# An output add moved between two kinds' taps, and the last round's fillers re-dealt

## The reference

```
yc = conv(qkv);  qkv = silu(yc)
M = where(stril, (k_beta @ k.T) * decay, 0);  T = inv(I + M)
v_new = v_i - kcd_i @ state
out_i = (q_i * exp(g_i)) @ state + attn @ v_new
state = state * exp(g_last) + (k_i * exp(g_last - g_i)).T @ v_new
s = (norm_w * rms(core) * silu(z)) @ W_out.T
x + s * silu(ffn(xn))
```

## Time and profile before

| | |
|---|---|
| median of three timed runs | 2303.93 us |
| the profiled execution | 2307.89 us |
| its span, first to last instruction | 2306.1 us |
| PE, DVE, ACT, POOL busy in the span | 94%, 71%, 57%, 74% |
| mean granted TensorE clock | 0.986 |
| chain that ended last: PE, DVE, ACT, issue | 66%, 17%, 9%, 5% |

### The profile page before, as it was taken

The page is one execution under the profiler, slowest core; times in us unless marked ns, Lnnn a source line. Parts: engine busy times, 40 slices in busy tenths (PEclk is TensorE's granted clock), DMA queues, the critical chain, the costliest instruction groups (busy, mean ns, idle before and its releaser), DMA issues.

```text
span 2306.1 us, 76444 instructions
## 1 busy us (share of the span) xinstructions
PE 2178.9 (94%) x32208; PEld 1671.9 (72%) x32208; DVE 1641.1 (71%) x3307; ACT 1311.1 (57%) x3141; POOL 1709.9 (74%) x1774
## 2 busy tenths in 40 slices
PE   3799999999999999999999999999999999998898
PEld 2687777777777777777777777777777777776554
DVE  6777777777777777777777777777877677776322
ACT  3666655666566655666556555666665566664111
POOL 2787888888877888888877788888877788888100
PEclk8899999999999999999999999999999999999999
DMA  3211110111111110111111110111111102111100
GB/s 91 56 42 34 46 37 25 31 46 37 46 32 35 46 37 22 33 46 37 46 32 35 46 30 26 37 46 37 41 37 34 35 21 46 37 37 42 38 19 19
DMA packets 70951, 87.45 MB, mean 38 GB/s; under 512 B 16721, under 2 KB 39377, under 8 KB 70609
## 3 DMA queue, kind: packets, MB, share of 16 engines
q1 hardware_dynamic: 70608, 82.55, 14.0%
HBM read 77.45 MB, written 5.08 MB: 36 GB/s over the span
## 4 chain that ended last, share of the span: by engine, by line
PE 66%; DVE 17%; ACT 9%; issue 5%; POOL 2%; DMA 1%; DVEq 0%; POOLq 0%; SPq 0%; ACTq 0%
DVE cacc L1016 10%; PE ps_two L429 10%; PE ps_p L675 8%; PE ps_state L429 5%; PE ps_p L612 4%; PE ps_two L454 4%; PE ps_state L636 3%; PE ps_p L585 3%; PE ps_p L620 3%; PE ps_p L503 3%; PE ps_state L503 2%; ACT qg L790 2%; PE ps_p L724 2%; DVE acc L1281 2%; PE ps_two L664 2%
## 5 line engine op out<-in xcount | busy, mean ns | idle before, releaser
L1351 POOL TENSOR_TENSOR Sd<-St,el 128x512 f32<-128x512 f32 x192 | 201.3, 1048 | 276.6 <-DVEq L1253 276.6
L1390 POOL TENSOR_SCALAR Kg<-idx_s,lutb 128x134 f32<-128x134 int32 x480 | 355.7, 744 | 27.1
L1232 DVE TENSOR_SCALAR Vn<-ps_p,bR 128x128 f32<-128x128 f32 x512 | 168.2, 350 | 225.8 <-PE ps_p L585 151.9
L1016 DVE SCALAR_TENSOR_TENSOR cacc<-ps_state,cw,cacc 128x1022 f32<-128x1022 f32 (+2 forms) x192 | 244.4, 1273 | 15.5 <-DVE cacc L1016 7.6
L675 PE MATMUL ps_p<-w_o,hT 128*128 128x256 f32 x992 | 244.5, 390 | 7.1 <-ACT V L829 5.8
L1016 DVE SCALAR_TENSOR_TENSOR cacc<-ps_two,cw,cacc 128x1022 f32<-128x1022 f32 (+2 forms) x192 | 244.9, 1275 | 5.3 <-DVE cacc L1016 0.5
L429 PE MATMUL ps_state<-xnT,w_qkv 128*128 128x256 f32 x1024 | 234.2, 382 | 5.9 <-DVEq L1021 5.9
L429 PE MATMUL ps_two<-xnT,w_qkv 128*128 128x256 f32 x1024 | 236.4, 384 | 0.0
L429 PEld LDWEIGHTS ps_state<-xnT,w_qkv 128*128 128x128 f32 x1024 | 193.6, 192 | 32.6 <-DVEq L1021 6.3
L922 ACT ACTIVATE P<-ps_p 128x128 f32<-128x128 f32 x256 | 67.2, 277 | 260.6 <-PE ps_p L590 260.6
L675 PEld LDWEIGHTS ps_p<-w_o,hT 128*128 128x128 f32 x992 | 182.1, 191 | 43.6 <-issue 19.9
(11 more groups left out here) (195 smaller groups left out, 5388.6 us busy)
## 6 DMA issues: line engine op xcount, KB each, us to landing
qg<-g_scratch SPq DMA_DIRECT2D x64, 512.0 KB, 7.3
g_st<-g_scratch SPq DMA_DIRECT2D x64, 256.0 KB, 5.5
w_qkv<-in_wqkvz SPq DMA_DIRECT2D x16, 512.0 KB, 3.8
w_z<-in_wqkvz SPq DMA_DIRECT2D x16, 256.0 KB, 3.2
w_o<-in_wout SPq DMA_DIRECT2D x16, 256.0 KB, 2.9
idx_s<-in_idx SPq DMA_DIRECT2D x32, 67.0 KB, 1.8
fw_scratch<-looked_up SPq DMA_DIRECT2D x32, 67.0 KB, 2.7
Kg<-in_x SPq DMA_DIRECT2D x2, 1024.0 KB, 5.9
```

What stands on the lines that cost most here:

```text
L1016: dve.scalar_tensor_tensor(dst, both[n][:, :, 0:S - t], cw[:, kind, 3 - t:4 - t], dst, ALU.mult, ALU.add).then_inc(s["taps"], 1)
L1232: dve.tensor_scalar(Vn[:, cur, b], bank[:, 0:P], bR[:, R.par, b, c:c + 1], None, ALU.mult).then_inc(done, 1)
L1351: pool.tensor_tensor(Sd[:, :, :, :], St[:, c % 2, :, :, :], el[:, R.par, :, :, c].unsqueeze(3).broadcast_to([P, BB, RATIO, P]), ALU.mult). ...
L1390: m = pool.tensor_scalar(slots[k], idx_s[:, :], float(k), lutb[:, k:k + 1], ALU.is_equal, ALU.mult)
```

## The change

1. In rounds 1 to 30 DVE adds output quarter 3 between the taps of kind 2 and those of kind 3, not after them.
2. In the last round PE computes output quarters 0, 1 and 2 ahead of the first products of the inversion, and DVE adds them there. Quarter 2 goes to bank 7 and quarter 3 to bank 5; hidden unit 1, whose banks are 6 and 7, waits for quarter 2 to be read.
3. At the last round's end the four output quarters are interleaved with hidden units 3, 4 and 5 of the FFN's first group: PE computes quarters 0 and 1, unit 3, the turning of quarter 3, quarter 2, unit 4, quarter 3, and unit 5 once unit 3 has been multiplied. The quarters use banks 0 and 2 instead of 0 and 1. ACT and DVE take the units in the same order, before the loops of the FFN and DVE's wait for x.

```diff
-AHEAD = {0: 0, 1: 6, 2: 0}
+AHEAD = {0: 0, 1: 6, 2: 0, 3: 4, 4: 6, 5: 4}
+IN_LEVELS = 3
+OUT_LAST = {(5, 1): (3,)}
...
-    outs = [] if first else spread([("out", 0), ("out", 1), ("out", 2), ("ot3", 0), ("out", 3)], (5, 4, 5, 4, 4))
+    outs = [] if first else spread([("out", 0), ("out", 1), ("out", 2), ("ot3", 0), ("out", 3)], (5, 4, 5, 4, 4) if nxt else (5, 4, 7, 4, 5))
...
-    end = [] if nxt else spread([("end", i) for i in range(4)], (0, 1))
+    end = [] if nxt else spread([("end", i) for i in range(4)], (0, 2))
...
                 if R.before() is not None:
-                    outputs(R, "out", R.before(), 0)
+                    for t in range(1 if R.nxt else 3):
+                        outputs(R, "out", R.before(), t)
...
+                        if f == 1 and j == 0:
+                            wait_read(pe, R, "out", 2)
...
-                    turn_back(R, 3)
-                    for t in range(4):
-                        outputs(R, "end", R, t)
+                    outputs(R, "end", R, 0)
+                    outputs(R, "end", R, 1)
+                    for j in range(2):
+                        gate_up(3, 3, 0, j, AHEAD[3])
+                    turn_back(R, 3)
+                    outputs(R, "end", R, 2)
+                    for j in range(2):
+                        gate_up(4, 4, 0, j, AHEAD[4])
+                    outputs(R, "end", R, 3)
+                    pe.wait_ge(s["ff_h"], 4)
+                    for j in range(2):
+                        gate_up(5, 5, 0, j, AHEAD[5])
...
                 scale_last(R)
+                if not R.nxt:
+                    for f in range(IN_LEVELS, FT):
+                        gated_unit(f, f, AHEAD[f])
...
                 if of is not None:
                     gated(of, 3)
+                if R.nxt and of is not None:
                     outputs(R, "out", of, 2)
                 if R.nxt:
                     taps(R, 2, (1, 2, 3))
-                    taps(R, 3, (1, 2, 3))
                 else:
                     hidden(2, 2, AHEAD[2])
                 if of is not None:
                     outputs(R, "out", of, 3)
+                if R.nxt:
+                    taps(R, 3, (1, 2, 3))
...
                     gated(R, 2)
+                    outputs(R, "end", R, 0)
+                    outputs(R, "end", R, 1)
                     gated(R, 3)
-                    for t in range(4):
-                        outputs(R, "end", R, t)
+                    outputs(R, "end", R, 2)
+                    hidden(3, 3, AHEAD[3])
+                    outputs(R, "end", R, 3)
+                    hidden(4, 4, AHEAD[4])
+                    hidden(5, 5, AHEAD[5])
```

More of the change, by code:

```diff
@@ L557, in beside @@
                 if R.before() is not None:
-                    for t in OUT_AT.get((lv, half), ()):
+                    for t in (OUT_AT if R.nxt else OUT_LAST).get((lv, half), ()):
                         outputs(R, "out", R.before(), t)
@@ L563, in beside @@
                         if not R.nxt:
-                            pe.wait_ge(s["ff_h"], len(AHEAD))
+                            pe.wait_ge(s["ff_h"], IN_LEVELS)
                     zproj(R, i)
@@ L1196, in invert @@
                 if of is not None:
-                    outputs(R, "out", of, 0)
+                    for t in range(1 if R.nxt else 3):
+                        outputs(R, "out", of, t)
                 second_products(R, 4, 2)
@@ L1204, in invert @@
                     hidden(1, 1, AHEAD[1])
-                if of is not None:
+                if R.nxt and of is not None:
                     outputs(R, "out", of, 1)
```

## The result

The changed kernel takes 2246.77 us (median of 4 runs, 2245.33 to 2248.87), the kernel before 2304.13 us in the same comparison (2302.78 to 2312.45).

The account below looks back on a forecast made before the run. PE was taken to bound the kernel, waiting in 30 rounds for DVE's late add and stalling seven times. Terms 26.7 + 4.9 + 0 + 9.2 = 40.8 us gave 2263.1 us from the 2303.93 median; range 2248 to 2285.

Parts of the forecast that it names:

- Change 1, the stalls: Seven stalls inside `keys_through`: fetch gets ahead of the `w_qkv` load, so four even ones shrink to odd size, 4.9 us gained.
- My second rival: All seven `keys_through` stalls go, as PE's sequencer can run ahead during z products: 16.0 us, time 2252.0; chance 0.10.
- Change 1, the thirty rounds: Rounds 1 to 30: `keys_through` starts 0.97 us earlier, ACT's lateness costs 0.08; 0.89 a round, 26.7 us gained.
- Change 2: Last round's first phase: same PE work in another order, no gap to fill; 0 gained.
- Change 3: Last round's end: idle time between units and quarters filled, slow clock gone, first down product 9.2 us earlier.
- ACT in PE's place: Rounds: the recurrence's first products already hang on ACT's Kg copies, each round loses 0.07 us; time 2296.8, chance 0.10.
- More stalls: Rounds: the 0.97 us pause lets fetch keep up, without it further rounds stall 2.29 us each; up to 2320.7, chance 0.04.
- Quarter 3's bank not full: Rounds: DVE waits for PE's quarter 3, taps come late, only the end gains; 2294.7 us, chance 0.04.
- Instruction fetch: Stalls in `keys_through`: by the skill's rule of mostly hidden block crossings the stall term would be 0, time 2268.0.

Follow-up runs that it names:

- the end alone: Kernel before with only the last round's output quarters interleaved with hidden units 3 to 5: 2294.81 us, ratio 0.9963.
- gates first: Changed kernel with ACT taking the SiLU of z products 0 to 2 before the SiLU of kind 3: 2239.64 us, ratio 0.9709.
- held kernel: Any kernel whose PE waits just before `keys_through`; the kernel before with the head's transposes made three times, 128 instructions more, ran once at 2319.71 us.

## Why the prediction was wrong

- **Change 1, the stalls: the step that failed.** I wrote that the instructions "queue behind" the `w_qkv` load, and took the difference between even and odd stalls, 4.9 us; by the traces the disturbed rounds were worth 29.0. Two things were wrong, the cause and the price. The cause: the stalls come from the wait itself, and go with it, odd ones too. My second rival said so, at 0.10, and "nothing shows how far the sequencer runs ahead" was my argument against it. The traces do show it, in the DMA view of the stretch just ahead of `keys_through` in round 16. In the kernel before (1147.3 to 1149.6 us, L577 at 1149.60) only data moves, and the instruction packet comes in the stretch after the earlier trace rows:

```profile
q1 hardware_dynamic: 144, 0.07, 12.5%
```

After the change (1126 to 1128.3 us, L582 at 1128.32) the packet is there ahead of it:

```profile
q1 hardware_dynamic: 152, 0.07, 12.1%
q8 instruction: 1, 0.02, 2.4%
```

  The same holds of all seven rounds: the packet starts 1.0 to 2.7 us behind the first product of `keys_through` in the kernel before, and 1.2 to 1.7 us ahead of it in the same rounds after. When it is asked for no view shows. One case could have been read before any run: round 0 of the kernel before has no late add to wait for, and in the 1.2 us ahead of its first product (114.9 to 116.1) nothing moves but

```profile
q8 instruction: 1, 0.02, 5.6%
```

- **The price of the stalls.** Even the rival stopped at 16.0 us, the idle time that the view puts before the stalled matmul. The rounds lost 29.0, the seven alone 26.0. In round 16 of the kernel before, the half z product behind the stalled matmuls took 2.07 us where an undisturbed round has 1.12, and that second delay is in no row on L577:

```profile
1154.95 2.07 PE L454 MATMUL ps_two<-xnT,w_z 128*128 128x512 f32 x2
```

  It is the clock. PE had stood idle for 2.68 us, and as it resumes its granted clock falls from 1.00 to 0.50 (2.4 to 1.2 GHz). The stretch, in the columns of the earlier trace rows:

```profile
1153.93:1157.34 3.41, 3.32 (x31) 1.70 (x33) 0.00 (x0) 1.08 (x2) 0.00 (x0) 0.50 0.00 0
```

  Such a slow stretch stands behind five of the seven stalls, in rounds 8, 16, 24, 25 and 26. Beyond 64.07 us and its stall's idle time, each of these rounds is 1.8 to 2.1 us longer; rounds 9 and 17, whose clock stays at 1.00, are so by 0.3 and 0.4 us. From these rounds' lengths the clock's share is, by estimate, 5 x 1.5 = 7.5 us. One pair shows it alone: round 26 stalls for the same 3.00 us at the same place in the kernel before and with the end alone, but with the end alone the clock stays at 1.00, and the round takes 67.50 us instead of 69.08. The kernel before first:

```profile
1812.16 0.33 PE L577 MATMUL ps_state<-XW,Kg 64*64 64x64 f32 x3 [3.00 <-issue]
1812.41 1.83 PE L454 MATMUL ps_two<-xnT,w_z 128*128 128x512 f32 x2
```

```profile
1808.29 0.33 PE L578 MATMUL ps_state<-XW,Kg 64*64 64x64 f32 x3 [3.00 <-issue]
1808.55 1.13 PE L455 MATMUL ps_two<-xnT,w_z 128*128 128x512 f32 x2
```

  Measured from L577 to L577, as the undisturbed 64.07 us was, the price had been there to read. With it the rival gives 26.7 + 29.0 + 9.2 = 64.9 us; the two traces are 62.6 apart, the medians 57.4.

- **Change 1, the thirty rounds.** The forecast was 0.89 us a round; 0.77 was measured. The mechanism was right: L582 starts at the z products' end, the second batch's banks are free in time, ACT's wait before the copies is used up, and L590 is late by 0.13 us (0.08 forecast). What I missed is a second hand-over from ACT: the half z product needs bank 0, which the SiLU of z product 1 frees, and that SiLU stands behind the later SiLU of kind 3. The half z product starts at 1003.93 where 1003.78 was due (1.06 us behind the second batch's first matmul, as with gates first: 1000.81 against 999.75). Gates first removes both, and the round gains 0.25 us more.

- **Change 2.** The forecast was 0. One pair of traces shows 0.3 us lost, another 0.4 gained.

- **Change 3.** The forecast was 9.2 us; it gave 9.5 in the traces and 10.1 alone. Idle time and slow clock both went, as the sum had them.

- **The rivals.** ACT in PE's place: it took 0.25 us of the 1.02 that a round can gain (64.07 against 63.05 with gates first), not all. More stalls: there were none. Quarter 3's bank not full: DVE did not wait for PE there.

- **Instruction fetch.** The Trainium skill ("Runtime: NRT & Kernel Launch", section "Instruction fetch mechanics") calls the crossing into the next block mostly hidden. In `keys_through` that held in 25 of 32 rounds of the kernel before, and in all of the changed one. In the other seven a wait of 0.98 to 1.15 us was followed at once by 256 instructions that take 2.04 us, and the stall came after 95 to 126 of their 128 matmuls.

## What to carry to other kernels

A wait on PE can cost more than its own idle time when dense small matmuls follow it. Here taking 30 waits of 0.97 us away gave 23 us, and 29 more by what had followed them in a few rounds: the next packet of instructions had come 1.0 to 2.7 us behind the wait's end instead of ahead of it, PE had stood idle again, and behind five of these stalls its clock had fallen to 0.50. Price a recurring stall by the length of the disturbed period against an undisturbed one, not by the idle time before one instruction, and read the granted clock behind it. Before reordering an engine to free a bank sooner, look for a bank that is already free: here it gave 6 us more, and ACT was not made late.

## What the runs showed of the hardware

- In a held kernel the rounds that stall follow the code's place: 128 more instructions ahead moved them from 8, 9, 16, 17 and 24 to 26 to 3, 4, 11 to 13, 20, 21 and 28 to 30.
- In the seven rounds that stalled the packet with the next instructions started 1.0 to 2.7 us behind the end of the wait, and 1.2 to 1.7 us ahead of the same matmul once there was no wait.
- After a stall of 3.00 us the clock fell to 0.50 in the kernel before and stayed at 1.00 with the end alone; the round took 69.08 us and 67.50.
- A 512 KB load issued just before a stall lengthens it: 2.68 us with it, 1.85 us with the load moved behind `keys_through`, both in round 16.
- Executions with stalls spread further: 2300.75 to 2313.7 us over 23 runs of the kernel before, 2238.45 to 2240.18 over 4 of the fastest, which has none.
